# Both ends of a transformer layer on one core: order of the first stack loads, of the last chunk's down products, and of GpSimd's final work

## The reference

```
x = layernorm(x + attention(x))        # 16 heads of 32, causal, ALiBi bias, Wq Wk Wv Wo with biases
logits = x @ Wr + br                   # 4 experts, top 1, weight = its softmax probability
h = silu(x @ Wg[e]) * (x @ Wu[e])      # 512 -> 2048, only the chosen expert's output is kept
out = layernorm(x + weight * (h @ Wd[e]))   # 2048 -> 512
```

## Time and profile before

| | us |
|---|---|
| median of three runs | 1272.7 |
| the profiled execution | 1271.8 |
| its span, first to last instruction | 1270.0 |
| TensorE busy in it | 1170.9 (92%) |
| VectorE, ScalarE, GpSimd busy | 768.9, 569.9, 307.1 |

### The profile page before, as it was taken

One profiled execution on the slowest core, in us unless ns is written; L12 is line 12 of the kernel. 1 busy time (PEld: TensorE's weight loads), 2 busy tenths in 40 slices (PEclk: granted clock), 3 DMA queues, 4 the chain that ended last, 5 costly groups with the idle time before them and its releaser, 6 DMA issues.

```text
span 1270.0 us, 27816 instructions
## 1 busy us (share of the span) xinstructions
PE 1170.9 (92%) x8697; PEld 1066.8 (84%) x8697; DVE 768.9 (61%) x1978; ACT 569.9 (45%) x1395; POOL 307.1 (24%) x443
## 2 busy tenths in 40 slices
PE   6998999999899987499999999999999999999993
PEld 5887878888888875498998899889989988998882
DVE  2576776677767775456646654664566466546564
ACT  4577765675666673053323332323233233323343
POOL 4400210110020123343303311330232033113326
PEclk9999999999999997599999999999999999999996
DMA  8222223222322240261223132222313232322202
GB/s 258 74 51 70 72 67 98 54 69 67 93 51 63 67 122 34 73 185 48 86 68 91 52 93 67 59 76 68 101 47 88 68 86 55 94 69 60 75 27 108
DMA packets 109685, 100.11 MB, mean 79 GB/s; under 512 B 12847, under 2 KB 81839, under 8 KB 109552
## 3 DMA queue, kind: packets, MB, share of 16 engines
q1 hardware_dynamic: 104784, 87.85, 24.6%
q0 software_dynamic: 3040, 9.18, 2.2%
q10 hardware_dynamic: 1728, 1.31, 0.3%
HBM read 64.74 MB, written 9.18 MB: 58 GB/s over the span
## 4 chain that ended last, share of the span: by engine, by line
PE 74%; POOL 6%; DVE 5%; ACT 4%; issue 4%; DMA 4%; SPq 2%; ACTq 0%; DVEq 0%; POOLq 0%
PE bank L788 34%; PE bank L566 14%; PE bank L813 9%; PE bank L704 4%; POOL up_lo L1432 4%; PE bank L687 4%; PE bank L800 2%; PE bank L676 2%; DMA up_raw<-in_Wu_dram 2%; SPq L476 2%; ACT probs L896 1%; PE bank L664 1%; PE bank L713 1%; POOL out_dram L1486 1%; DVE probs L1133 1%
## 5 line engine op out<-in xcount | busy, mean ns | idle before, releaser
L788 PE MATMUL bank<-up_hi,xsT_hi 128*128 x1216 | 356.4, 293 | 9.7 <-POOL up_lo L1432 9.0
L788 PE MATMUL bank<-up_lo,xsT_hi 128*128 x1216 | 344.8, 284 | 0.0
L788 PE MATMUL bank<-up_hi,xsT_lo 128*128 x1216 | 344.7, 283 | 0.0
L1432 POOL TENSOR_TENSOR up_lo<-up_raw,up_hi 128x256 fp32r<-128x256 f32 x241 | 169.9, 741 | 483.5 <-ACT up_hi L928 483.3
L1274 DVE SCALAR_TENSOR_TENSOR h_tok<-bank,row_weight,silu 128x128 f32<-128x128 f32 x304 | 93.5, 347 | 299.0 <-ACT silu L992 299.0
L788 PEld LDWEIGHTS bank<-up_hi,xsT_hi 128*128 128x128 f32 x1216 | 233.2, 192 | 16.2 <-issue 16.0
L788 PEld LDWEIGHTS bank<-up_hi,xsT_lo 128*128 128x128 f32 x1216 | 233.8, 192 | 0.2
L788 PEld LDWEIGHTS bank<-up_lo,xsT_hi 128*128 128x128 f32 x1216 | 233.3, 192 | 0.0
L992 ACT ACTIVATE silu<-bank 128x256 f32<-128x256 f32 (+1 forms) x160 | 59.6, 373 | 373.8 <-PE bank L788 373.8
L1291 DVE TENSOR_TENSOR y<-bank,y 128x512 f32<-128x512 f32 x295 | 198.9, 689 | 0.4
L896 ACT ACTIVATE probs<-probs,neg_max 128x512 f32<-128x512 f32 (+3 forms) x256 | 136.5, 558 | 57.3 <-DVE neg_max L1133 56.3
(11 more groups left out here) (168 smaller groups left out, 2090.9 us busy)
## 6 DMA issues: line engine op xcount, KB each, us to landing
up_raw<-in_Wg_dram SPq DMA_DIRECT2D x64, 256.0 KB, 3.1
up_raw<-in_Wu_dram SPq DMA_DIRECT2D x64, 256.0 KB, 3.8
down_raw<-in_Wd_dram SPq DMA_DIRECT2D x64, 256.0 KB, 2.7
k_stack<-qk_hi SPq DMA_DIRECT2D x128, 64.0 KB, 2.0
q_stack<-qk_hi SPq DMA_DIRECT2D x128, 64.0 KB, 2.0
k_stack<-qk_lo SPq DMA_DIRECT2D x64, 64.0 KB, 2.0
q_stack<-qk_lo SPq DMA_DIRECT2D x64, 64.0 KB, 2.0
x_tok<-in_x_dram SPq DMA_DIRECT2D x3, 1024.0 KB, 6.4
```

The source lines that it names most:

```text
L788: mm = pe.matmul(bank[:, n * 2 * P:(n + 1) * 2 * P], a[:, s, k, :], up_w[w][k][:, :, :].rearrange("p a f -> p (a f)")[:, bass.ds(at, 2 * P ...
L1432: pool.tensor_tensor(up_w[1][k][:, e, :], up_raw[:, idx % NUPS, k, :, :].rearrange("p g f -> p (g f)"), up_w[0][k][:, e, :].bitcast(F32), ...
```

## The change

Three edits. First, `DOWN_WITH` gives each up pair from the third on one pair of down products, so that pair 0's come after up pair 2 rather than 4, and no up pair has two. For that the last chunk's four down weights are split two and two, ahead of the gates of pairs 0 and 1. Second, GpSimd does the deviation of pair `pr` before the stores of pair `pr - 1`. Third, group 0's stacks are loaded part by part: the hi parts of K wait only for ScalarE's K, the lo part for VectorE's K, and likewise for Q. The order is K of head 0, K of head 1, Q of head 0, Q of head 1, then K and Q of head 2, K and Q of head 3. For the later groups the order within Q is hi, hi, lo and no longer hi, lo, hi; nothing else is changed there.

```diff
-DOWN_WITH = {4: (0,), 5: (1,), 6: (2, 3), 7: (4, 5), 8: (6,), 9: (7,)}
+DOWN_WITH = {2: (0,), 3: (1,), 4: (2,), 5: (3,), 6: (4,), 7: (5,), 8: (6,), 9: (7,)}
 ...
+            def load_part(h, n, low):
+                rows = slice(h * HD, (h + 1) * HD)
+                stack, parts = {WK: (k_stack, (qk_hi, qk_hi, qk_lo)), WQ: (q_stack, (qk_hi, qk_lo, qk_hi))}[n]
+                for r, part in enumerate(parts):
+                    if (part is qk_lo) == low:
+                        sp.dma_start(stack[r * HD:(r + 1) * HD, h, :].bitcast(F32),
+                                     part[rows, n, :].bitcast(F32)).then_inc(s_stack[h], 16)
+
+            def load_first_stack(h, n, job):
+                sp.wait_ge(s_side_act, plan.act_number[job])
+                load_part(h, n, False)
+                sp.wait_ge(s_side_dve, plan.number[job])
+                load_part(h, n, True)
 ...
-            for h in range(GH):
-                load_stacks(0, h)
+            for h in (0, 1):
+                load_first_stack(h, WK, ("K", 0))
+            for h in (0, 1):
+                load_first_stack(h, WQ, ("Q", 0))
+            for h in (2, 3):
+                load_first_stack(h, WK, ("K", 0))
+                load_first_stack(h, WQ, ("Q", 0))
 ...
                     if c == NC - 1:                      # ScalarE; on VectorE ahead of gate_pair too
+                        if pr < 2:
+                            split_down(c, 2 * pr)
+                            split_down(c, 2 * pr + 1)
 ...
-                    if pr < NE:
+                    if pr < NE and c < NC - 1:
                         split_down(c, pr)
 ...
-            for together in [DOWN_WITH[pr] for pr in range(NE, NPAIR)] + [DOWN_AFTER]:
-                for pr in together:
-                    final_deviation(pr)
-                for pr in together:
-                    for s in PAIRS[pr]:
-                        final_store(s)
+            for pr in range(NPAIR):
+                final_deviation(pr)
+                for s in PAIRS[pr - 1] if pr else ():
+                    final_store(s)
+            for s in PAIRS[NPAIR - 1]:
+                final_store(s)
```

More of the change, by code:

```diff
@@ L467, in load_x @@
                 sp.dma_start(x_tok[:, (b + 1) % 2, :, :], x_rows[b]).then_inc(s_x[b % 2], 16)
+            def load_part(h, n, low):
[10 more added lines that the diff above has]
+                load_part(h, n, True)
             def load_stacks(g, h):
                 sp.wait_ge(s_side_dve, max(done("K", g), done("Q", g)))
[L471 to L477, removed]
+                sp.wait_ge(s_scores, scores_count(g - 1, h))
+                for n in (WK, WQ):
+                    load_part(h, n, False)
+                    load_part(h, n, True)
             def store_x1(t):
@@ L1322, in vector @@
                             split_rows(s)
+                    if pr < 2 and c == NC - 1:
+                        split_down(c, 2 * pr)
+                        split_down(c, 2 * pr + 1)
                     gate_pair(c, pr)
```

## The result

The changed kernel takes 1257.44 us (median of six runs, 1255.55 to 1261.71) beside 1270.04 us for the kernel before (six runs, 1268.08 to 1274.9). The ratio is 0.9897 with a 95% interval of 0.9873 to 0.9922. Two later comparisons of the same code gave 0.9923 (0.9894 to 0.9952) and 0.9899 (0.9881 to 0.9917). The forecast was 1265.0 us with a range of 1260 to 1271.

A forecast was written before the change was run, and what follows sets the result against it. TensorE, busy 92%, bounds the kernel; SyncE's issue rate bounds the second hole, GpSimd the end. Front -1.8 and end -5.0 sum to -6.8: span 1263.2, plus 1.8 around it 1265.0 us, range over the cases 1260 to 1271.

The forecast's parts named there:

- The end: Last chunk: down products a step ahead and GpSimd's new order give -5.0 us, bounds -2.5 and -6.5.
- The steps of 4.49: Last chunk on TensorE: an up pair with one pair of down products takes 4.49 us, six such steps from pair 1's transposes.
- GpSimd's chain: Last chunk: GpSimd's deviations and stores follow without a hole after pair 6's deviation, ending at 1260.3 against 1265.34.
- The rival of slower stores: Last chunk: stores beside VectorE's work slow from 1.27 to over 1.7 us, GpSimd sets every step; up to 1277.5, chance 0.07.
- a pitch over 1.5: Last chunk on GpSimd: stores standing more than 1.5 us apart would show the forecast wrong.
- The front: Start of the kernel: 0.4 - 1.84 - 0.32 = -1.8 us, bounds +0.6 and -5.0.
- K's hi from 18.4, last part at 33.6: SyncE's issue of group 0's stacks: starts at 18.4, ends at 33.6 against 37.55, 3.9 us earlier.
- Head 0 is 0.4 later, for three more DMAs stand ahead of it: First hole on TensorE: head 0's stacks land 0.4 us later, behind x and head 1's K in the queue.
- The holes of 1.84 and 0.32 go whole: Second hole: TensorE's waits for VectorE's bias step (1.84 us) and an exponential (0.32 us) vanish.
- I expect that it still does, since the hole stays: After the first hole: TensorE still runs 3.5 us at a granted clock of 0.52.
- the clock's 1.8 us: Front: price of the half clock after the first hole, 1.8 us, counted only in the -5.0 bound.
- the front opens: Rival at the start: head 0 at its early bound, clock stays high, front -5.0 instead of -1.8, 1261.8 us; chance 0.15.

The follow-up runs named there:

- end_only: Kernel before with the new last chunk and GpSimd order alone, stacks loaded as before: 1264.86 us, ratio 0.9952 to the kernel before.
- the table alone: Kernel before with the new table of down products and two-by-two split, GpSimd's order as before: 1267.1 us, ratio 0.9962 to the kernel before.
- pool_only: Kernel before with GpSimd's new order alone, down products where they were: 1270.13 us, ratio 0.9989 to the kernel before.
- front_only: Kernel before with the new loading of group 0's stacks alone: 1265.66 against 1270.21 us, ratio 0.9954.
- after_x_late: Changed kernel with the second sequence's 1 MB of x loaded behind group 0's stacks: 1260.3 us, ratio 0.9902 to the kernel before.
- after_third: Changed kernel, nothing altered, in its third comparison with the kernel before: 1258.19 us, ratio 0.9899.
- after: Changed kernel with all three edits, first comparison with the kernel before: 1257.44 against 1270.04 us, ratio 0.9897.
- after_again: Changed kernel, nothing altered, in its second comparison with the kernel before: 1261.5 us, ratio 0.9923.
- act_head3: Changed kernel with head 3's six stack DMAs issued by ScalarE between its V copies, not by SyncE: 1259.42 us, ratio 0.9908 to the kernel before.

## Why the prediction was wrong

**The end: right.** Forecast -5.0 us, measured -5.33 in the last chunk (62.34 to 57.01) and 6.1 (3.8 to 8.4) in the time of `end_only`. The steps of 4.49 were 4.48; pair 8's transposes came 38.88 us after the chunk's start, forecast 1241.91 - 1203.00 = 38.91. GpSimd's chain came out the same: pair 6's deviation done 41.4 us after the start (forecast 41.5), last store's end 57.0 (57.3). The two-by-two split cost nothing. The rival of slower stores did not decide: a store takes 0.97 us or, right behind a deviation, 1.07 to 1.36. Its sign, a pitch over 1.5, did appear three times (1.64 to 1.66, as from 1235.69 to 1237.33), some 0.8 us in all over the usual 1.38, and the sum held. What I had not seen is that each edit needs the other; the table alone is worth 3.8 and the order alone nearly nothing. In `pool_only` GpSimd's first deviation is at 19.3 us after the chunk's start, as before (19.3), and from 28.7 us on it waits only 2.3 us in all until the last store. With the new table it starts at 13.1.

**The front: wrong, by the term that failed.** I wrote -1.8 and it is -5.8 (-3.7 to -8.0). Step by step:

- *K's hi from 18.4, last part at 33.6*: nearly. That end is 15.9 us after the first `qk_hi` began; in the changed kernel and `front_only` the last issue ends at +16.4 to +17.0 (+19.8 before), since one or two issues took longer. So it is 2.9 to 3.4 us earlier and not 3.9.
- *Head 0 is 0.4 later, for three more DMAs stand ahead of it*: not borne out. I had the first scores at 29.3 to 29.9, which is +11.6 to +12.2. They stand at +10.1 to +10.5 without the change and +10.3 to +10.8 with it in the usual kind, at +11.60 and +11.83 in the rarer one. The half of it that was right is that x ahead in the queue holds them up; `after_x_late` shows it, with first scores 0.76 us earlier or more. The rule of the Trainium skill ("DMA: Bandwidth & Descriptors", "Queues, rings and completion order"), that each engine consumes its ring in order, agrees with this. That three more transfers then cost a further 0.4 us I had worked out from one row; the profiles allow some 0.2, and can't tell that from nothing.
- *"The holes of 1.84 and 0.32 go whole"*: wrong in the profiles of the new loading with the usual first hole, where 1.30 to 1.68 us of the second one stay and ScalarE's stall, for which I had asked under 0.7, is 3.14; right in the rarer one (`after_third`).
- *"I expect that it still does, since the hole stays"*, of the half clock: this is the step that failed, together with the 2.16 us that I took for all that the second hole could give back. I left the clock's 1.8 us out of the sum. The 3.5 us that ran at 0.52 run at 1.00 in `after`, and no half-clock stretch comes before 180 us in `after`, `after_again` and `front_only`. The rival "the front opens" had it, with 0.15. It gave the front 5.0 us and so nearly the right size, with head 0 at its early bound, 28.2 or +10.5. The usual first scores are there, but without the change too, so that is not where its gain comes from.

Behind the last two stands one error. I took one execution's holes for the kernel's. The first scores wait for stacks that stand behind x in the queue; if x lands late, TensorE reaches the second hole late and it is short, and if it lands in time the second hole is 4.7 to 5.1 us long, because its end is set by the last stack's issue and landing and not by TensorE. So whatever the first hole does, the scores after hole 2 stand at +23.3 to +24.4 in all kernels with the old loading. Had I asked what ends the second hole in each case, I would have seen that a short one depends on how long x's load takes. With the new loading the usual second hole is 1.3 to 2.1 us, and the clock stays whole: some 3.2 us earlier at that place (+20.1 to +21.0 for +23.3 to +24.1), and one to three us of clock. Where the rarer kind meets the changed kernel, the forecast comes nearly true (`after_third`, 1.8 us); but that kind is three of sixteen profiles.

**The rest.** With the measured sizes -1.8 and -5.0 become -5.8 and -5.3, 11.1 us; the ratios 0.9897, 0.9923 and 0.9899 are 13.1, 9.8 and 12.8 us. The stretch in the expert part that was 4.6 us shorter in the first pair of profiles (661.5 to 656.9) is no part of the change: among the sixteen profiles it runs from 655.5 to 664.1 us, with 656.7 and 664.1 in two kernels that are the one before but for throwaway products at the start. The five longest (660.7 us and more) are those in which TensorE waits 7.1 to 8.6 us for GpSimd's `up_lo`; in the others it waits 3.5 to 6.1. In four of the five a half-clock stretch or two falls in the expert part, in the others none. I passed it over as fixed, and it varies by more than my whole forecast. The medians of before, 1272.7 for the first three runs and 1270.0 to 1271.8 later, account for 1 to 2.7 us of what my number was off by.

What stays open: how much of the front's 5.8 us the half clock is (2 to 3 us by two comparisons of other kernels whose intervals are as wide, at most 1.7 by the granted clocks of `front_only`), why stretches of 3.4 us follow holes of 1.67 and 1.9 to 2.0 us and not others of that length, why x's load and the expert part differ from run to run, and whether the 1 to 2 us which `act_head3` takes from the front reach the end.

## What to carry to other kernels

Read a hole by what sets its two ends. If the later end is set by a queue and the earlier one by a load whose time varies, its length in one profile says little, and two or three profiles are worth more than a finer sum. A wait on TensorE costs more than its length when it is long enough for the half clock to follow, and less than its length can be regained when the next wait has a fixed end: `after_x_late` took 0.8 to 1 us from the first hole and lost it in the second. When two engines share a step, compare each one's own work for a step before moving anything: here GpSimd's 4.80 us against TensorE's 4.48 was what the table alone left, 1.5 of the 5.3 us.

## What the runs showed of the hardware

- TensorE's idle time of 2.47 us or more before 60 us was followed by 3.4 or 6.8 us at a granted clock of 0.5 in eight of nine cases (2.47, 2.59, 2.69, 3.11, 3.36, 4.74, 4.92 and 5.12 us; not after 2.67), and of 2.06 us or less by none but one (3.4 us after 1.67). Near 90 us it was followed so in four of sixteen, with holes of 1.92 to 1.99 us and not with 2.02 to 2.19.
- In the five profiles with 6.8 us (before 60 us) the clock fell 0.3 to 1.5 us before the hole had ended (at 38.7 in the hole from 35.22 to 40.14), in the four with 3.4 us 0.3 to 1.7 us after its end.
- A 1 MB load in SyncE's queue took 10.4 to 13.8 us from issue to landing in fourteen executions, and the first use of the stacks queued behind it came 1.2 to 2.8 us after that landing in all of them.
- Throwaway products in an idle hole made a kernel 2.3 us faster (0.9982, 0.9968 to 0.9996), with 2.8 us less of missing clock (standard error 1.2).
- Identical instruction streams of 660 us in the expert part differ by up to 8.6 us between the sixteen profiled executions (655.5 to 664.1).
